# Attention gated by top-2 experts on one core: three split products for every chunk, more maxima early, fewer per block

## The reference, cut to what matters

```python
xn = layernorm(x)
# attention: 16 heads of 8 features, over xn normalised once more
q, k, v = split_heads(layernorm(xn) * ln_w + ln_b) @ W_qkv + b_qkv
attn = softmax(q @ k.T / sqrt(8));  s = xn + (attn @ v) @ W_proj + b_proj
# experts: 8 of them, hidden size 512, the top two of the router count
weights = softmax(where(logits >= second_largest(logits), logits, -inf))
h = gelu(xn @ W1[e] + b1[e]);  f = sum_e weights[:, e] * (h @ W2[e] + b2[e])
out = x + s * silu(f)
```

## Time and profile before

| | |
|---|---|
| median of 3 runs | 1085.9 us (1085.82 to 1093.49) |
| the profiled execution itself | 1088.44 us |
| its span, first to last instruction | 1086.7 us |
| TensorE (PE), busy | 1026.8 us, 94% |
| VectorE (DVE), busy | 889.2 us, 82% |
| ScalarE (ACT), busy | 860.9 us, 79% |
| GpSimd (POOL), busy | 370.2 us, 34% |

### The profile page before, as it was taken

How to read it: one execution, slowest core, us unless ns; L and a number is a source line. 1 busy time by engine, 2 the same in 40 slices (tenths; PEclk the granted TensorE clock), 3 DMA queues, 4 the chain that set the end, 5 groups by cost and what they waited for, 6 DMA issues and landing times.

```text
span 1086.7 us, 17511 instructions
## 1 busy us (share of the span) xinstructions
PE 1026.8 (94%) x5865; PEld 441.9 (41%) x5865; DVE 889.2 (82%) x1621; ACT 860.9 (79%) x1158; POOL 370.2 (34%) x554
## 2 busy tenths in 40 slices
PE   5898999999999999999999999999989999999997
PEld 3675666666666666663221222212212112221222
DVE  5656887888878888765999999989989999999943
ACT  6776767676767667667888998989879989888985
POOL 4795656767676666553001000001000001000010
PEclk9899999999999999998999999999999999999998
DMA  6333132414141322424212121212122212122113
GB/s 185 117 92 84 50 99 34 121 31 125 36 117 36 94 59 45 106 63 110 52 40 69 39 57 38 70 38 57 40 53 53 56 40 55 48 61 55 25 25 83
DMA packets 109267, 72.16 MB, mean 66 GB/s; under 512 B 31741, under 2 KB 93882, under 8 KB 109178
## 3 DMA queue, kind: packets, MB, share of 16 engines
q1 hardware_dynamic: 109178, 71.05, 25.8%
HBM read 53.12 MB, written 15.59 MB: 63 GB/s over the span
## 4 chain that ended last, share of the span: by engine, by line
PE 30%; SPq 8%; ACT 7%; DVE 4%; DMA 3%; issue 2%; POOL 0%; ACTq 0%; DVEq 0%; POOLq 0%
PE psum L1023 14%; PE psum L1002 8%; PE psum L980 7%; ACT p_ring L856 6%; DVE neg_max_half L1283 3%; SPq L464 3%; SPq L468 2%; SPq L453 2%; DMA den<-o_sb 1%; SPq L438 1%; DMA q_stack<-neg_max_dram 1%; PE psum L1051 1%; ACT o_sb L847 1%; PE psum L1065 0%; DMA rden_dram<-rden 0%
## 5 line engine op out<-in xcount | busy, mean ns | idle before, releaser
L856 ACT ACTIVATE p_ring<-psum 128x1024 f32<-128x1024 f32 x512 | 494.9, 1028 | 64.0 <-PE psum L1002 58.7
L1283 DVE TENSOR_REDUCE neg_max_half<-psum 128x1 f32<-128x512 f32 x768 | 481.3, 680 | 39.3 <-PE psum L980 32.5
L1023 PE MATMUL psum<-p_ring,v_sb 128*9 128x512 f32 x2048 | 270.4, 600 | 0.2 <-ACT o_sb L847 0.2
L1309 DVE TENSOR_REDUCE neg_max_half<-psum 128x1 f32<-128x512 f32 x256 | 171.4, 685 | 74.7 <-PE psum L967 74.1
L818 ACT ACTIVATE h_hi<-psum,cols 128x512 fp32r<-128x512 f32 x192 | 132.4, 690 | 117.3 <-PE psum L931 116.8
L980 PE MATMUL psum<-k_max_stack,q_max_stack 48*128 48x512 bf16 x768 | 204.3, 382 | 17.5 <-DVE neg_max_half L1283 17.3
L1002 PE MATMUL psum<-q_stack,k_stack 51*128 51x512 bf16 x1024 | 200.6, 388 | 8.9 <-ACT p_ring L856 4.2
L680 POOL TENSOR_TENSOR h_lo<-h_split,h_hi 128x512 fp32r<-128x512 f32 x128 | 165.9, 1300 | 120.5 <-ACT h_split L821 120.5
L1002 PEld LDWEIGHTS psum<-q_stack,k_stack 51*128 51x128 bf16 x1024 | 49.7, 93 | 309.2 <-ACT p_ring L856 284.8
L630 POOL CAST neg_max_parts<-neg_max_rest 128x16 bf16<-128x16 f32 x32 | 6.5, 202 | 491.9 <-DVE neg_max_rest L1292 491.8
L929 PE MATMUL psum<-xn_t_hi,w_lo 128*128 128x512 f32 x256 | 145.2, 567 | 0.4 <-ACT h_split L821 0.3
(11 more groups left out here) (126 smaller groups left out, 974.1 us busy)
## 6 DMA issues: line engine op xcount, KB each, us to landing
expert_w_bc<-expert_w_dram SPq DMA_DIRECT2D x64, 256.0 KB, 5.0
k_rows_dram<-qk_parts SPq DMA_DIRECT2D x24, 256.0 KB, 3.1
q_max_stack<-q_rows_dram SPq DMA_DIRECT2D x64, 96.0 KB, 2.5
k_max_stack<-k_rows_dram SPq DMA_DIRECT2D x64, 96.0 KB, 2.6
q_stack<-q_rows_dram SPq DMA_DIRECT2D x64, 96.0 KB, 2.5
k_stack<-k_rows_dram SPq DMA_DIRECT2D x64, 96.0 KB, 2.5
q_rows_dram<-qk_parts SPq DMA_DIRECT2D x8, 384.0 KB, 2.6
q_stack<-neg_max_dram SPq DMA_DIRECT2D x192, 2.0 KB
```

Of the source, the lines that this page charges most:

```text
L856: act.activation(p_sb[:, n % PR, a, :, :].rearrange("p h t -> p (h t)"), scores_bank[s % 2], ACT.Exp, scale=SCALE).then_inc(S("P"), 1)
L1023: i = pe.matmul(o_bank[at:at + VR, :], v_sb[:, b * KT + kt, 2 * (p % PB) + hh, :], p_sb[:, n % PR, a, hh, :], start=(kt == 0), stop=(kt == ...
L1283: dve.tensor_reduce(mx[:, p % MXR, c, hh * NT + t:hh * NT + t + 1], ring_bank(("max", u)), AX.X, ALU.max, negate=True).then_inc(S("R"), 1)
L1309: dve.tensor_reduce(mx[:, p % MXR, c, hh * NT + t:hh * NT + t + 1], early_bank[m % 2], AX.X, ALU.max, negate=True).then_inc(S("R"), 1)
```

## The change

1. Expert phase: all four chunks of an expert take the split way. `w_full` and `h_full`, the float32 matmul and its single gelu are gone; chunk 3 has three matmuls, two gelus, and a subtraction on POOL. POOL's `newton` is cut in three, one iteration per slot.
2. `EARLY_PAIRS` is 10 instead of 8: 320 maxima in the same slots (36 + 27m/40), 704 in attention.
3. Attention: exactly three maxima a block, from block 2 to block 236: two after `scores(2n)` into banks 5 and 6, which one `tensor_reduce` reads together (128 x 2 x 512), one after `scores(2n+1)` into bank 7.
4. Transfers: a pair's maxima are stored by two DMAs instead of one and loaded by two instead of six; the row sums move in one instead of four, `rden_t` is filled by two instead of four. `head_rden` comes one block later, and `rden_in` two blocks later.

```diff
-        EARLY_PAIRS = 8
+        EARLY_PAIRS = 10
+        TRIO = 3
...
+        def block_units(n):
+            first = TRIO * (n - MAX_FROM)
+            if first < 0:
+                return (), ()
+            at = [min(len(SINGLES), first + k) for k in (0, 2, 3)]
+            return range(at[0], at[1]), range(at[1], at[2])
...
-        EARLY_AT = [HT + 4 + (27 * m) // 32 for m in range(EARLY)]
+        EARLY_AT = [HT + 4 + (27 * m) // 40 for m in range(EARLY)]
...
             for hh in range(2):
-                src = m_dram[p, :, VC * hh:VC * (hh + 1)].rearrange("(b i t) c -> i t b c", b=P // VC, t=NT)
-                for i in range(PARTS):
-                    row = HALF * hh + QROWS + i
-                    sp.dma_start(q_s[row:row + 1, slot, :].rearrange("a (t b c) -> a t b c", t=NT, c=VC), src[i:i + 1])\
-                        .then_inc(S(f"m_ld{slot}"), 16)
+                sp.dma_start(q_s[HALF * hh + QROWS:HALF * hh + SROWS, slot, :], m_dram[p, hh, 0:PARTS, :])\
+                    .then_inc(S(f"m_ld{slot}"), 16)
...
-            for t in range(4):
-                sp.dma_start(den[t * n:(t + 1) * n, slot, :],
-                             o_sb[VC * t + DH:VC * t + VR, slot, :].rearrange("a (n k) -> a n k", n=n))\
-                    .then_inc(S(f"den{slot}"), 16)
+            sp.dma_start(den[:, slot, :], o_sb[DH:P:VC, slot, :].rearrange("a (n k) -> a n k", n=n))\
+                .then_inc(S(f"den{slot}"), 16)
...
-                return {4: [newton(g, 1)], 10: [newton(g, 2)], 21: [rest(0)], 22: [rest(1)],
-                        25: [third(0)], 26: [third(1)]}
+                plan = {21: [rest(0)], 23: [rest(1)], 26: [third(0)], 28: [third(1)]}
+                for n in range(NEWTON):
+                    plan[4 + n] = [newton(g, 1, n)]
+                    plan[10 + n] = [newton(g, 2, n)]
+                return plan
...
-                        if not split(i):
-                            wait(pe, "hf", g, E, e + 1)
-                            pe.matmul(o, w2f[:, e, :], hf[:, e % 2, :], start=False, stop=True).then_inc(S("m2"), 1)
-                            return
...
                         pe.matmul(o, w2l[:, e, ws], hh[:, at, :], start=(c == 0), stop=False)
                         pe.matmul(o, w2h[:, e, ws], hh[:, at, :], start=False, stop=False)
                         hl_done(pe, g, i)
-                        pe.matmul(o, w2h[:, e, ws], hl[:, at, :], start=False, stop=False).then_inc(S("m2"), 1)
+                        pe.matmul(o, w2h[:, e, ws], hl[:, at, :], start=False, stop=(c == HC - 1)).then_inc(S("m2"), 1)
...
-                ring_free(pe, ("max", u))
+                elif u >= TRIO and u % TRIO != 1:
+                    pe.wait_ge(S("R"), EARLY + u - (1 if u % TRIO == 0 else 2))
...
+                if len(at) == 2:
+                    dve.tensor_reduce(flat[:, at[0]:at[1] + 1:at[1] - at[0]],
+                                      psum[:, 5 * TG:7 * TG].rearrange("p (u t) -> p u t", u=2), AX.X, ALU.max,
+                                      negate=True).then_inc(S("R"), 2)
...
-                if p > 0 and kt == 5:
+                if p > 0 and kt == (6 if p < PAIRS - 1 else 5):
                     head_rden(p - 1)
```

More of the change, by code:

```diff
@@ L544, in _ @@
                         sp_max_rows(sp, p)
[L545 to L546 removed]
+                for p in {2: [2], 4: [5], 6: [8]}.get(g, []):
+                    sp_max_rows(sp, p)
                 if g + 1 < NG:
@@ L685, in experts @@
                 for i in range(HT):
-                    if split(i) and not by_vector(i):
+                    if not by_vector(i):
                         plan.setdefault(i, []).append(low_h(i))
@@ L1333, in head_rden @@
                 slot = p % 2
-                dve.wait_ge(S(f"den{slot}"), 64 * (p // 2 + 1))
+                dve.wait_ge(S(f"den{slot}"), 16 * (p // 2 + 1))
                 if p > 1:
```

223 lines of the change are left out of this document (90 added, 133 removed).

## The result

The changed kernel takes 1101.15 us (median of 7 runs, 1096.5 to 1102.31); the kernel before took 1086.13 in the same session (7 runs, 1085.67 to 1094.27). The ratio is 1.0107, 95% interval 1.0073 to 1.0141: slower by about 1%, where 2% faster was forecast. The profiled execution took 1101.44 us, its span is 1099.7.

A forecast was written before the change was run, and what follows sets the result against it. ScalarE was taken to bound attention, TensorE the expert phase with VectorE second. Terms -41 + 4 (plain TensorE work) + 15 + 3 = -19 us against the profiled 1088.4, or 1067 us against the median; forecast 1055 to 1079, range 1048 to 1085.

The forecast's parts named there:

- 54 x (2.69 - 1.95) = 40 us: the size agrees: Attention: 54 blocks with a fourth maximum, 2.69 us against 1.95, were taken to explain ScalarE's missing 42 us.
- Rival (d): Attention: the fourth maximum isn't why ScalarE waits, but, say, PE's fixed order; 1091 us, chance 0.05.
- Part 4: Transfers: DVE's 4.9 us for `den` goes, already inside the 17.74; eight fewer DMAs a pair delay nobody: 0.
- Part 3: Attention: three maxima a block, two in one pass of 1.17 us; ScalarE sets 16.3 us a pair: -41 us.
- Rival (b): Attention: the pass over two banks holds PE up 0.08 us a block, taking back 19 us; 1086 us, chance 0.13.
- Part 1: Expert matmuls: splitting 64 chunks saves 11 us on PE; gelus and subtractions beside it cost +3, bounds -2 and +10.
- The cover: Experts: three slots, some 5 us, between a chunk's up and down; two gelus and a subtraction need 2.7 us.
- a few us: Experts: if VectorE and GpSimd two-input SBUF instructions exclude each other, the sum comes out a few us later.
- -2 (newton in thirds holds up no subtraction for long): Experts: lower bound, -2 us, of the +3 us allowed for work beside the split matmuls.
- The 0.8 us a group: Experts: the first newton ends 0.8 us after DVE's arrival, behind slot 5's subtraction, lengthening each group by 0.8 us.
- Part 2: Experts: ten early pairs add +15 us of PE work and +15 us of stalls, 2.5 a group; stall bounds 0 and 36.
- Rival (c): Experts: VectorE sets the phase, bursts passed on whole, PE's clock falls; 8 us a group gives 1100 us, chance 0.07.

## Why the prediction was wrong, point by point

**What bounds attention.** ScalarE does, once it is fed: of the 16.32 us a pair, all but 0.3 (7.9 us of waits for scores over 29 pairs) are its sixteen exponentials, a copy and the short gaps between them. The total was right: -42 for a forecast of -41. Its makeup was not. The step "54 x (2.69 - 1.95) = 40 us: the size agrees" took an agreement of sizes for a cause. Without the fourth maxima alone 23 us went. Rival (d), that they aren't why ScalarE waits, was right by half.

**Part 4, transfers at 0.** Wrong: -12 alone, and -22 once ten pairs are early (45 - 23), with the later `rden_in` in both. "Eight fewer DMAs a pair on SP delay nobody" was said of a queue whose timeline I had not read. The earlier trace rows had the hint, a wait for `den`, and I took it for a matter of its own.

**Part 3, the pass.** Its duration was 1.226 us, between my bounds (1.06 to 1.25) and above the 1.17 taken. Rival (b), that it holds up TensorE, didn't come. But two single ones do as well, so nothing of the -41 was its doing.

**Part 1, split chunks at -11 + 3.** This is the step that failed. With the cut `newton` they cost +31 us in place of -8 (23.1 + 7.9). The matmuls were right, as far as busy time tells: with all chunks split and the subtraction short TensorE is busy 407.9 us between the closes of the first and the eighth group, with the float32 chunk 416.6, 8.7 less for 56 chunks. The term for what is beside them was mis-sized: +3, with a bound at +10. It came to 42 (31 + 11): 25 to 26 for the subtractions, at 0.40 us each, 7.9 for `newton`, and about 9 whose cause stays open. The cover that I named (5 us of slots against 2.7 of work) did hold: TensorE waits 1.4 us in all for GpSimd's `h_lo` in 104:560. I priced the subtraction by whether its own result is in time, and the price came up elsewhere: it goes with the length of VectorE's instructions, and reaches TensorE as late maxima. The paragraph that named the Trainium skill pointed this way and stopped at "a few us". The length of the second gelu was free, as forecast.

**`newton` in thirds.** The bound "-2 (newton in thirds holds up no subtraction for long)" looked at the wrong side: what is held up is `newton`. It cost 7.9 us, 5.2 of it in the first group, which I had read nowhere. The 0.8 us a group that I gave it in part 2 was the right mechanism (0.4 a group measured, 64.2 to 64.6); the first group was missing.

**Part 2, ten early pairs at +15 and +15.** Measured alone: +24.0, so 9 us of stalls for a forecast that, less newton's share of 5, was 10. Right in size. In part wrong in cause: 5.8 of the 9 went when the stores of maxima came earlier, and bursts, as far as an uneven spread can avoid them, were worth 4 at most.

**The sum.** The expert phase was forecast 22 us longer and came out 55 longer: 39 more than forecast for part 1 with `newton` (31 against -8), 6 less for part 2 (24 against 30). TensorE's wait for early maxima was 30.8 us, above my 15 to 25; a group took 64.6, just inside the 65 at which I had called the prediction wrong; the first group's +13.6 us was hardly in any term. Rival (c), VectorE sets the expert phase, at 0.07, names the right engine, and its 1100 us hit the time by luck: it put 8 us a group on bursts passed on whole and on stops of TensorE of over 3 us. The phase lost 5.9 a group and 13.6 in the first, TensorE's longest wait for a maximum was 2.5 us, and VectorE was late more by GpSimd's doing than by its bursts.

## What to carry to other kernels

Price an instruction moved to an idle engine by what it does to its neighbours and to the other steps in that engine's list, not only by whether its own result is in time; adding 48 idle copies of it to a kernel without it measures this in one run. Read the timeline of the issuing queue before calling transfers free, above all where the change makes the rest faster. When the size of a cause agrees with the size of a wait, there may still be a second limit just below it that takes over.

## What the runs showed of the hardware

- A GpSimd subtraction of two 128x512 SBUF operands cost the kernel 0.40 us (a needed one, shortened) to 0.43 (one used by nobody, added); an addition with one operand, though longer (1506 ns against 1306), 0.20; three fills of the same area, 531 ns each, 0.23 to 0.28. VectorE's busy time for the same work rose by 26.6, 11.1 and 14.4 us for 48 of each, while its reductions from PSUM stayed at 683 or 684 ns.
- A reduction of 2 x 512 scores over two banks took 1226 ns, one of 512 takes 672 to 684: one pass in place of two saved 0.12 to 0.14 us of VectorE and nothing of the kernel's time.
- Where VectorE stood twice for a store, 13.3 us in all, TensorE's waits in 105:540 were 19.6 us against 14.4, and the eighth group closed 8.3 us later (532.4 against 524.1): more than the waits. TensorE's longest was 5.9 us, and the granted clock was 0.87 in 300:325, so part of that stretch ran at 1.2 GHz.
